# Moving the fold, the wide add and the result by one unit, and statistics and loads by one to four, in a software-pipelined convolution kernel

## The reference, cut to what matters

```python
def _gn(v, G=32, eps=1e-05):             # mean and variance over 2 channels x 56 x 56
    ...
    return ((g - m) / jnp.sqrt(s + eps)).reshape(v.shape)

def _L0_conv_ref(x, ...):
    h = lax.conv_general_dilated(jnp.sign(x), jnp.sign(dw_weight), ..., feature_group_count=C)
    h = jnp.sign(_bn(_prelu(h, prelu1_a), ...))
    h = jnp.einsum('bchw,oc->bohw', h, jnp.sign(pw_weight))
    return _bn(_prelu(h, prelu2_a), ...) + x

def _L1_conv_ref(x, W, b):               # involution: nine filters from x itself
    filters = jnp.einsum('bchw,oc->bohw', x, W) + b[None, :, None, None]
    ...
    return jnp.sum(patches * filters, axis=-1)

x = x + _L0_conv_ref(_gn(x), ...)
x = x + _L1_conv_ref(_gn(x), L1_conv_W, L1_conv_b)
```

## Time and profile before

| | before |
|---|---|
| time, median of 3 runs | 722.55 us (721.29 to 723.13) |
| span of the profiled execution | 720.7 us |
| busy: VectorE, GpSimd, ScalarE | 657.6 us (91%), 632.8 us (88%), 501.9 us (70%) |
| TensorE matmul busy | 609.0 us (85%), granted clock near full from 8% of the span on |
| chain that ended last, by engine | GpSimd 73%, idle issue 9%, VectorE 8% |
| folds: issue to landing, median | 10.2 us |

### The profile page before, as it was taken

How to read it: one execution, slowest core, us unless ns; L and a number is a source line. 1 busy time by engine, 2 the same in 40 slices (tenths; PEclk the granted TensorE clock), 3 DMA queues, 4 the chain that set the end, 5 groups by cost and what they waited for, 6 DMA issues and landing times.

```text
span 720.7 us, 18683 instructions
## 1 busy us (share of the span) xinstructions
PE 609.0 (85%) x8017; PEld 258.6 (36%) x8017; DVE 657.6 (91%) x982; ACT 501.9 (70%) x629; POOL 632.8 (88%) x328
## 2 busy tenths in 40 slices
PE   2649789888888989898998988889888889898897
PEld 1314333333334334343433334333333434342233
DVE  4949889999999999999999999999999999999886
ACT  6967896968678596868869686877859686734110
POOL 2004589999999999999999999999999999999996
PEclk9979999999999999999999999999999999999999
DMA  5247596998999899898989899899989987897984
GB/s 204 84 137 126 109 263 146 208 226 186 255 194 253 186 224 231 163 259 186 265 184 244 194 192 241 186 259 189 252 184 208 225 187 166 190 204 166 200 173 136
DMA packets 34279, 142.10 MB, mean 197 GB/s; under 512 B 3348, under 2 KB 11540, under 8 KB 32276
## 3 DMA queue, kind: packets, MB, share of 16 engines
q0 software_dynamic: 17232, 75.87, 59.1%
q1 hardware_dynamic: 16940, 65.03, 25.4%
q10 hardware_dynamic: 24, 0.00, 0.0%
HBM read 26.03 MB, written 25.69 MB: 72 GB/s over the span
## 4 chain that ended last, share of the span: by engine, by line
POOL 73%; issue 9%; DVE 8%; ACT 5%; PE 2%; DMA 2%; SPq 0%; POOLq 0%; DVEq 0%; ACTq 0%
POOL prod L402 29%; POOL ob L426 13%; POOL prod L415 11%; POOL prod L408 9%; POOL prod L384 7%; DVE prod L939 4%; POOL st L371 2%; ACT unused L601 2%; POOL st L369 1%; PE tap_ps L541 1%; DVE xb L913 1%; DMA xb<-in_x_dram 1%; PE tap_ps L498 1%; ACT ab L601 1%; ACT q L601 1%
## 5 line engine op out<-in xcount | busy, mean ns | idle before, releaser
L939 DVE SCALAR_TENSOR_TENSOR prod<-tap_ps,bias,q 128x784 f32<-128x784 f32 x493 | 485.7, 1025 | 30.0 <-PE tap_ps L498 17.9
L498 PE MATMUL tap_ps<-q,w_t 64*64 64x392 f32 x2304 | 465.1, 502 | 52.1 <-DVE prod L939 26.3
L498 PE MATMUL tap_ps<-mirror,w_t 64*64 64x392 f32 x2304 | 459.9, 502 | 0.0
L498 PEld LDWEIGHTS tap_ps<-q,w_t 64*64 64x64 f32 x2304 | 153.8, 133 | 253.4 <-DVE prod L939 174.4
L402 POOL TENSOR_TENSOR prod<-prod 128x2352 f32<-128x2352 f32 x45 | 233.7, 5194 | 0.0
L601 ACT ACTIVATE ab<-tap_ps,col 128x784 bf16<-128x784 f32 x128 | 120.8, 995 | 50.9 <-PE tap_ps L541 50.3
L541 PE MATMUL tap_ps<-signs,dw_diag 64*64 64x392 bf16 x2304 | 133.1, 335 | 17.0 <-DVE prod L939 12.5
L498 PEld LDWEIGHTS tap_ps<-mirror,w_t 64*64 64x64 f32 x2304 | 139.3, 133 | 0.2 <-issue 0.2
L426 POOL TENSOR_TENSOR ob<-prod 128x784 f32<-128x784 f32 x63 | 132.3, 2100 | 4.5
L541 PEld LDWEIGHTS tap_ps<-signs,dw_diag 64*64 64x64 bf16 x2304 | 70.2, 108 | 105.4 <-issue 54.5
L415 POOL TENSOR_TENSOR prod<-prod 128x784 f32<-128x784 f32 x45 | 104.2, 2315 | 0.0
(11 more groups left out here) (118 smaller groups left out, 335.0 us busy)
## 6 DMA issues: line engine op xcount, KB each, us to landing
prod<-prod POOLq DMA_DIRECT2D x63, 1176.0 KB, 10.2
out_dram<-ob SPq DMA_DIRECT2D x31, 784.0 KB, 5.9
xb<-in_x_dram SPq DMA_DIRECT2D x15, 1568.0 KB, 12.4
mirror<-q SPq DMA_DIRECT2D x64, 203.0 KB, 4.5
xb<-in_x_dram SPq DMA_DIRECT2D x2, 784.0 KB, 5.6
out_dram<-ob SPq DMA_DIRECT2D x2, 392.0 KB, 2.3
prod<-in_L_conv_W_dram SPq DMA_DIRECT2D x1, 288.0 KB
prod<-in_L_conv_pw_weight_dram SPq DMA_DIRECT2D x1, 32.0 KB
```

What stands on the lines that cost most here:

```text
L498: mm = pe.matmul(rows3(tap_ps[to, slot, side, 0:CH]), w_t[own, k, :], moving, start=True, stop=True)
L939: v.scalar_tensor_tensor(place.rearrange("p j (a b) -> p j a b", b=WD), psum.rearrange("p j (a b) -> p j a b", b=WD), s_(t, B4) if k == 4 ...
```

## The change

Only numbers change: the due units in `COURSE`, `EARLY` and `PROLOGUE`, and six delays. All instructions stay; their order changes where the new numbers pass one another.

```diff
 COURSE = {
-    'load': -115,
+    'load': -111,
...
- 'mean0': -72,
+    'mean0': -71,
...
- 'rstd0': -65,
- 'scales0': -61,
- 'inv_z': -56,
+    'rstd0': -66,
+    'scales0': -60,
+    'inv_z': -58,
...
- 'job3': -26,
- 'sum1': -16,
- 'mean1': -15,
- 'square1': -12,
+    'job3': -27,
+    'sum1': -18,
+    'mean1': -16,
+    'square1': -14,
...
 EARLY = {
...
-     'inv_z': -60,
-     'ratio': -60,
+        'inv_z': -63,
+        'ratio': -59,
...
-     'job1': -64,
+        'job1': -65,
...
-     'inv_z': -36,
-     'ratio': -36,
+        'inv_z': -41,
+        'ratio': -35,
...
-     'job0': -42,
+        'job0': -39,
...
-FOLD_DELAY = 4
-EARLY_ADD_DELAY = 14
+FOLD_DELAY = 5
+EARLY_ADD_DELAY = 13
 MEAN_DELAY = 12
-WIDE_ADD_DELAY = 21
-LATE_ADD_DELAY = 22
+WIDE_ADD_DELAY = 20
+LATE_ADD_DELAY = 23
...
-TAKE_DELAY = 13
+TAKE_DELAY = 16
 DW_OVER = 4
 
-OUT_DELAY = 23
+OUT_DELAY = 24
```

More of the change, by code:

```diff
@@ L996 @@
 COURSE = {
-    'load': -115,
- 'sum0': -74,
- 'mean0': -72,
- 'sign0': -69,
- 'square0': -66,
- 'var0': -63,
- 'rstd0': -65,
- 'scales0': -61,
- 'inv_z': -56,
[L1006 to L1009, removed]
- 'job3': -26,
- 'sum1': -16,
- 'mean1': -15,
- 'square1': -12,
[L1014 to L1018, removed]
+    'load': -111,
+    'sum0': -74,
+    'mean0': -71,
+    'sign0': -69,
+    'square0': -66,
+    'var0': -63,
+    'rstd0': -66,
+    'scales0': -60,
@@ L1019 @@
+    'inv_z': -58,
+    'ratio': -54,
+    'job0': -56,
+    'job1': -45,
+    'job2': -33,
+    'job3': -27,
+    'sum1': -18,
+    'mean1': -16,
+    'square1': -14,
+    'var1': -11,
+    'rstd1': -9,
+    'q0': -11,
+    'q1': -3,
+    'inverse': -8,
 }
 EARLY = {
[L1021 to L1027, removed]
-     'inv_z': -60,
-     'ratio': -60,
-     'job0': -65,
-     'job1': -64,
[L1032 to L1048, removed]
-     'inv_z': -36,
-     'ratio': -36,
[L1051 to L1071, removed]
-     'job0': -42,
-     'job1': -37,
-     'job2': -32,
-     'job3': -27},
+    0: {
+        'sum0': -68,
+        'mean0': -100,
+        'sign0': -68,
+        'square0': -67,
+        'var0': -66,
+        'rstd0': -64,
+        'scales0': -62,
+        'inv_z': -63,
+        'ratio': -59,
+        'job0': -65,
+        'job1': -65,
+        'job2': -59,
+        'job3': -58,
+        'sum1': -47,
+        'mean1': -48,
+        'square1': -47,
+        'var1': -44,
+        'rstd1': -47,
+        'q0': -44,
+        'q1': -43,
+        'inverse': -41},
@@ new lines @@
+    1: {
+        'sum0': -100,
+        'mean0': -100,
+        'sign0': -83,
+        'square0': -82,
+        'var0': -82,
+        'rstd0': -79,
+        'scales0': -74,
+        'inv_z': -41,
+        'ratio': -35,
+        'job0': -39,
+        'job1': -29,
+        'job2': -24,
+        'job3': -18,
+        'sum1': -9,
+        'mean1': -10,
+        'square1': -9,
+        'var1': -9,
+        'rstd1': -11,
+        'q0': -8,
+        'q1': -7,
+        'inverse': -6},
+    2: {
+        'sum0': -61,
+        'mean0': -58,
+        'sign0': -56,
+        'square0': -53,
+        'var0': -49,
+        'rstd0': -54,
+        'scales0': -46,
+        'inv_z': -46,
+        'ratio': -45,
+        'job0': -39,
+        'job1': -37,
+        'job2': -32,
+        'job3': -27},
@@ L1079 @@
     'bias': -49,
[L1080 to L1086, removed]
+    'turn_w': -44,
+    'copy_w': -45,
+    'signs_rest': -42,
+    'square_0': -61,
+    'square_1': -53,
+    'square_2': -53,
+    'square_3': -47,
 }
```

## The result

The changed kernel takes 725.15 us (median of 5 runs, 724.13 to 726.36) beside 722.82 (721.29 to 723.86) for the kernel before: a ratio of 1.0034, interval 1.002 to 1.0049. It is slower by 2.3 us, where 0.6 less was forecast: above the forecast's own range (719.8 to 724.1), inside the wider one (717.5 to 726), and on the other side of the time before. The profiled execution took 724.13 with a span of 722.3, 1.6 more than the span of before, so its trace shows two thirds of the loss.

A forecast was written before the change was run, and what follows sets the result against it. GpSimd, in a circle with VectorE (u21 to u5, fold, `final`), was taken to set the tile's 41.34 us. Terms 2.8 - 2.4 - 0.8 - 0.5 + 0.3 = -0.6 us took 722.55 to 722.0; range 717.5 to 726.

The forecast's parts named there:

- Step 1, cover: On GpSimd, `add_early` ahead of Q1's fold leaves `final`'s wait for `add35` uncovered: 14 x 0.20 = 2.8 us lost.
- Steps 2 and 3: On VectorE, `mean0` behind the second product gains 2.4 us; `mean1` ahead of u21 gains 0.8 us.
- The rivals on these steps: VectorE's wait bounds, 9.6 us back (5%); lost cover costs nothing (18%); lost cover costs 9.2 us by starts (10%).
- Step 4: Fourth job one unit earlier (TensorE, ScalarE, `x1_sum`): costs nothing; up to 0.5 us a tile if uncovered.
- One sign of the prediction: In the trace after, VectorE's wait at u21 was to be longer by some 0.7 us.
- Step 5: Q1's fold issued 1.8 us later on GpSimd's queue: landing costs nothing, fewer mirror-copy stalls gain 0.5 us.
- landing rival: Fold of Q1 lands too late for its wide add: 1 us for 13 tiles, 735 us; chance 5%.
- Step 6, the start: At the start, TensorE's order costs 0.55 us and `inv_z` gains 0.25: 0.3 lost, ends -0.3 and +1.5.
- The claim that most new numbers pass nobody: Fold, wide add, `add35`, `final`, stores and loads keep their places among their neighbours; no size given.
- The 0.55 for TensorE's order: At the start, job 1's Relu product precedes job 2's last convolution parts; 0.55 us of some 0.9 reaches the first product.
- the gain of 0.25 from `inv_z`: At the start, `inv_z` of tile 1 leaves the path between u0 and u1: 0.25 us gained.
- what it feeds rejoins: Tile 2's first job comes three units later, ScalarE does the same work without a pause; no cost given.

The follow-up runs named there:

- e10: Changed kernel with `EARLY` and the five GpSimd delays of the kernel before, and the load at -110 (behind the mirror copy): 718.92 us, ratio 0.9946.
- e13: Kernel before with the load at -110 instead of -115, behind the mirror copy: 721.90 us, ratio 0.9987.
- e9: Changed kernel with the load at -110 instead of -111, behind the mirror copy: 725.13 us, ratio 1.0032.
- e4: Changed kernel with `EARLY`, the load (-115) and the five GpSimd delays of the kernel before: 723.75 us, ratio 1.0014.
- e17: e9 with tile 2's `rstd0` back at -51 instead of -54: 723.75 us, ratio 1.0012.
- e19: e9 with job 1 of tile 0 back at -64 instead of -65: 723.67 us, ratio 1.0014.
- e18: e9 with tile 2's first job back at -42 instead of -39: 724.39 us, ratio 1.0024.
- e3: Changed kernel with the five GpSimd delays of the kernel before, load still at -111: 731.88 us, ratio 1.0127.
- e1: Changed kernel with `EARLY` and the load (-115) of the kernel before: 724.11 us, ratio 1.0027.
- e16: e9 with tile 2's `EARLY` numbers of the kernel before: 723.04 us, ratio 0.9999.
- e5: Changed kernel with job 1 of tile 0 back at -64 instead of -65: 724.49 us, ratio 1.0032.
- e14: e10 with the five GpSimd delays of the changed kernel: 722.01 us, ratio 0.9992.
- e11: e3 with the load at -115, ahead of the store as before: 723.59 us, ratio 1.0008.
- e12: Kernel before with the load at -111 instead of -115: 724.31 us, ratio 1.0029.

## Why the prediction was wrong

**Step 1, cover: right.** +0.20 at each Q3 in the trace, +3.1 in all against 2.8. **Steps 2 and 3: right together**, not priced apart. -3.0 against -3.2. A tile of e10 takes 283.73 - 242.66 = 41.07 us against 41.34, and 0.27 less is what the two steps had summed to (0.20 + 0.07):

```profile
242.66 3.96 POOL L408 TENSOR_TENSOR prod<-prod 128x1568 f32<-128x1568 f32 x1
...
283.73 3.93 POOL L408 TENSOR_TENSOR prod<-prod 128x1568 f32<-128x1568 f32 x1
```

The rivals on these steps fall: VectorE's wait did not give back its 9.6 us, and the cover cost neither 0 nor 9.2. **Step 4: not priced apart**, but it lies within the -3.0, and no wait of that size shows at u9 to u20 except 0.2 to 0.4 before the third `x1_sum` (4.5 us in 12 times in the list of the changed kernel above). One sign of the prediction did not come: VectorE's wait at u21 was to grow by some 0.7 us, and it is 1.1 in e10 against 1.0 in e13. The 0.70 of `mean0` went into the shorter tile (0.27), the wait before `x1_sum` (0.37) and u21 (0.1).

**Step 5: right in sign.** Its landing rival did not come: in the even part the folds of Q1 land 8.8 to 10.0 us after their issue, at least 2.6 ahead of their wide adds. The copy's stalls were worth 1.1 rather than 0.5 in the kernel before, and the medians show no loss to them in the changed kernel (725.15 against e9's 725.13). What was not seen is that the copy can bind by itself. In the changed kernel GpSimd is slow enough to hide it: VectorE waits 7.9 us there for `final` and 8.3 for TensorE, and in e9 16.7 for `final` alone. When GpSimd gets faster the copy binds: e4 gave up its gain there.

**Step 6, the start: the step that failed**, 3.1 by medians and 2.2 between two traces with the clock at 1.00 from 22 to 26 us, against 0.3; both lie beyond its upper end of 1.5. Three readings in it were wrong.

The claim that most new numbers pass nobody overlooked tile 2's `rstd0`. It passes the wide add of Q0, waits 9.45 us there, and delays a fold whose DMA then meets the mirror copy. The Trainium skill, "PSUM — Partial Sum Buffer", section "Engine vs sequencer instructions", calls GpSimd's queue strict FIFO; the trace agrees, by the 9.45 us idle in front of L369 with an add behind it that in e17 starts at 67.21.

The 0.55 for TensorE's order took VectorE's squares for a half cover. In the trace they cover nothing. ScalarE after, beside the second row:

```profile
26.59 3.69 ACT L601 ACTIVATE ab<-tap_ps,col 128x784 bf16<-128x784 f32 x4 [1.64 <-PE tap_ps L541]
```

Its 0.73 later start arrives at product u0 as 0.77 (48.33 against 47.56), and by Q3 it has grown to 1.3 (e19).

And the gain of 0.25 from `inv_z` did not come. VectorE from 46 us, after:

```profile
45.86 0.17 DVE L899 RECIPROCAL st<-st 128x1 f32<-128x1 f32 x1 [5.43 <-ACT st L601]
48.33 1.03 DVE L939 SCALAR_TENSOR_TENSOR prod<-tap_ps,bias,q 128x784 f32<-128x784 f32 x1 [2.31 <-PE tap_ps L498]
49.57 1.03 DVE L939 SCALAR_TENSOR_TENSOR prod<-tap_ps,bias,q 128x784 f32<-128x784 f32 x1 [0.20 <-PE tap_ps L498]
```

`inv_z` has left the path, but u1 waits for TensorE in its place, and follows u0 after 1.24 us instead of 1.27. The statement "what it feeds rejoins" about tile 2's first job is open: e18 leaves its price between 0 and some 1.6 us.

The conclusion of *no change* came from an even part that was well read and a start that was read from its neighbours on TensorE and VectorE, not from the order on each engine. Where the other 0.9 of the 3.1 us arise stays open.

## What to carry to other kernels

When an order by due times is changed, list for every engine who passes whom, the start included: a tiny instruction with a late input, put early on an engine that works in order, holds up all that stands behind it, DMA issues too. Where a big load and a small urgent copy share an issuing engine, the copy belongs ahead; here that move alone was worth 1.1 us, and together with the gain that it set free 3.9 (e10, faster than both kernels). And price pieces on a base whose occasional stalls are gone: before that e3 said the opposite of what its part was worth, and e1 and e4 showed a fraction of it.

## What had not been expected of the hardware

**TensorE's clock falls at other times in each execution.** Windows of 22 to 26 us: the columns are busy time of PE, PEld, DVE, ACT, POOL, then TensorE's granted clock. First e16, then e9, whose tables for that stretch are the same:

```profile
22.00:26.00 4.00, 2.97 (x64) 1.82 (x68) 3.85 (x10) 2.97 (x8) 0.00 (x0) 1.00 0.08 32
```

```profile
22.00:26.00 4.00, 3.38 (x48) 2.52 (x52) 3.85 (x8) 3.12 (x8) 0.34 (x1) 0.63 0.07 26
```

In e1, e5, e9 and e18 the granted clock was 0.57 to 0.69 there, partly at the lower level of 1.2 GHz; in the other profiles it was 1.00. The same four pointwise products, in e1 and in e14, which has the same tables there:

```profile
24.09 0.60 PE L560 MATMUL tap_ps<-ab,pw_a 64*64 64x392 bf16 x4
```

```profile
23.57 0.36 PE L560 MATMUL tap_ps<-ab,pw_a 64*64 64x392 bf16 x4
```

They take 0.60 us instead of 0.36, and product u0 of tile 0 came 0.6 to 1.2 us later than in a profile with the same order there and the clock at 1.00 (48.46 in e1, 47.62 in e14; 48.98 in e9, 48.37 in e16). Just before tile 15's first product TensorE idles 3.1 us for its mirror copy, and in e9 the next matmul takes 0.88 us, in e16 0.51:

```profile
672.84 0.88 PE L498 MATMUL tap_ps<-q,w_t 64*64 64x392 f32 x1 [3.14 <-DMA mirror<-q]
```

```profile
671.74 0.51 PE L498 MATMUL tap_ps<-q,w_t 64*64 64x392 f32 x1 [3.16 <-DMA mirror<-q]
```

Between Q57 and Q58, where this falls, e9 lost 1.0 us on the kernel before, and e16 gained 0.2. Why the clock falls in one execution and not in the next, these runs don't show. One profile is therefore good to about 1 us in the start and at the end, which is as much as a piece of the start costs.

**The spread is narrower with the copy ahead of the load.** The runs of the eight such kernels (e9, e10, e13, e14, e16 to e19; 6 to 12 runs each) lie within 1.1 to 3.3 us, those of e1, e4, e5, e11 and e12, whose copy comes behind it, within 4.6 to 6.9 (12 runs each), and those of the kernel before, run beside them, within 2.5 to 5.2 (23 to 33 runs).
